# Layer 0 of a graph network: filter taps split in batches through memory, and the elementwise work of a pair rearranged over four engines

## What is computed

```
norm = (row sums of adj + 1e-6) ** -0.5
f_hom = adj @ ((x @ theta) * norm) * norm
f_het = x @ W_h
gate  = sigmoid(x @ W_t + b_t)
out   = elu(gate * f_hom + (1 - gate) * f_het)
x1    = layernorm(x + out)
```

## Time and profile before

| | |
|---|---|
| median of 3 runs | 2163.93 us (2160.73 to 2166.66) |
| the profiled execution | 2163.51 us, its span 2161.7 us |
| TensorE, VectorE, ScalarE, GpSimd busy | 91%, 73%, 58%, 20% of the span |
| mean granted TensorE clock | 0.97 of 2.4 GHz |
| DMA over the span | 263 MB, 122 GB/s |

### The profile page before, as it was taken

The page is one execution under the profiler, slowest core; times in us unless marked ns, Lnnn a source line. Parts: engine busy times, 40 slices in busy tenths (PEclk is TensorE's granted clock), DMA queues, the critical chain, the costliest instruction groups (busy, mean ns, idle before and its releaser), DMA issues.

```text
span 2161.7 us, 36678 instructions
## 1 busy us (share of the span) xinstructions
PE 1971.6 (91%) x11270; PEld 1695.5 (78%) x11270; DVE 1583.6 (73%) x2837; ACT 1245.1 (58%) x2303; POOL 425.1 (20%) x370
## 2 busy tenths in 40 slices
PE   6888888887788879994999999999999999999997
PEld 5887777776688868883888888888888888888886
DVE  5999798798577766774777677777777777777674
ACT  6887687786455566663445454545454545545452
POOL 5887687685000000000000000000000000000000
PEclk9999999998899989996999999999999999999999
DMA  4556566555322268884212121212122121212110
GB/s 145 204 200 209 192 225 218 198 207 218 91 82 79 72 207 263 255 265 152 76 52 92 46 91 45 91 46 90 60 77 77 59 81 55 88 49 91 62 40 20
DMA packets 174943, 263.25 MB, mean 122 GB/s; under 512 B 13250, under 2 KB 125608, under 8 KB 170632
## 3 DMA queue, kind: packets, MB, share of 16 engines
q1 hardware_dynamic: 174856, 262.29, 35.9%
HBM read 174.16 MB, written 88.08 MB: 121 GB/s over the span
## 4 chain that ended last, share of the span: by engine, by line
PE 51%; issue 1%; DVE 1%; DMA 1%; ACT 1%; SPq 0%; POOLq 0%; POOL 0%; ACTq 0%; DVEq 0%
PE c_ps_g L1431 37%; PE c_ps_m L1412 4%; PE c_ps_s L1412 2%; PE c_ps_m L1440 2%; PE c_ps_y L1466 1%; PE c_ps_m L1442 1%; PE c_ps_y L1510 1%; PE c_ps_m L1510 1%; PE c_ps_s L1494 1%; PE c_ps_m L1441 1%; DMA c_yf<-y_spec 1%; PE c_ps_m L1511 0%; PE c_ps_y L1511 0%; DVE c_wi_l L1377 0%; ACT c_yo L1143 0%
## 5 line engine op out<-in xcount | busy, mean ns | idle before, releaser
L1215 POOL TENSOR_TENSOR c_rstd<-c_var_eps,c_neg_half 128x4 f32<-128x4 f32 x32 | 32.2, 1008 | 1131.7 <-DVE c_var_eps L1331 1131.7
L1431 PE MATMUL c_ps_g<-c_xh,c_wh_l 128*128 128x512 f32 x384 | 155.3, 405 | 0.0
L1431 PE MATMUL c_ps_g<-c_nh,c_wi_l 128*128 128x512 f32 x384 | 153.3, 399 | 0.0
L1431 PE MATMUL c_ps_g<-c_xl,c_wh_h 128*128 128x512 f32 x384 | 151.8, 395 | 0.0
L1431 PE MATMUL c_ps_g<-c_xh,c_wh_h 128*128 128x512 f32 x384 | 151.7, 395 | 0.0
L1431 PE MATMUL c_ps_g<-c_ch,c_wi_l 128*128 128x512 f32 x384 | 151.6, 395 | 0.0
L1431 PE MATMUL c_ps_g<-c_ch,c_wi_h 128*128 128x512 f32 x384 | 151.6, 395 | 0.0
L1431 PE MATMUL c_ps_g<-c_nh,c_wi_h 128*128 128x512 f32 x384 | 151.5, 395 | 0.0
L1431 PE MATMUL c_ps_g<-c_cl,c_wi_h 128*128 128x512 f32 x384 | 151.5, 395 | 0.0
L1431 PE MATMUL c_ps_g<-c_nl,c_wi_h 128*128 128x512 f32 x384 | 151.5, 395 | 0.0
L837 PE MATMUL m_ps<-m_wh,m_xl 128*128 128x256 f32 (+1 forms) x406 | 131.8, 325 | 20.7 <-DVE m_wl L817 20.6
(11 more groups left out here) (228 smaller groups left out, 6658.9 us busy)
## 6 DMA issues: line engine op xcount, KB each, us to landing
w_spec<-a_spec SPq DMA_DIRECT2D x32, 1088.0 KB, 11.0
m_w<-w_spec SPq DMA_DIRECT2D x34, 1024.0 KB, 7.5
a_xt<-in_x_t SPq DMA_DIRECT2D x64, 256.0 KB
a_xn<-in_x_n SPq DMA_DIRECT2D x64, 256.0 KB, 9.4
x_t<-a_x1t SPq DMA_DIRECT2D x64, 256.0 KB, 9.5
s_x<-x_t SPq DMA_DIRECT2D x64, 256.0 KB, 3.0
y_spec<-m_y SPq DMA_DIRECT2D x64, 256.0 KB, 5.6
c_x<-x_t SPq DMA_DIRECT2D x32, 512.0 KB, 4.1
```

What stands on the lines that cost most here:

```text
L1431: last = nc.tensor.matmul(out, stationary, moving, start=(count == 0), stop=(count == total - 1))
```

## The change

The taps no longer come in three copies per pair. In every fourth step SyncE loads the taps of four pairs at once over all 128 partitions (`tr`), ScalarE makes the high part (`th`) and VectorE the low part (`tl`), and three steps later SyncE stores high, low and high into a scratch tensor in memory (`taps_s`). From there it loads for each pair the 102 stacked rows (`gs`, now four buffers), in its step i for pair i-7. The spectra matmuls of a pair move from two steps after its load to six and seven steps after, and the stores of the finished spectra move back by as much.

The powers for the norm and for the normalisation become one power of four columns, in GpSimd's step i for pairs i-2 and i-6; the variance's epsilon is added by VectorE. The gate is written back to where it was in PSUM and read there by VectorE; the mix reads het in PSUM (the copy of het stays, for the difference). The normalisation becomes an instruction with three operands, the third a broadcast column. The clamp becomes a minimum with zero on GpSimd, and the exponential loses its sign. ScalarE's, GpSimd's, VectorE's and TensorE's instructions stand in another order in the step. In the product stage two semaphores of ScalarE become one, and VectorE's subtraction for x loses its own signal.

```diff
-def phase_a(nc, G, x_n, x_t, adj_t, w0, b_t, masks, x1_t, taps, dft_w, w_spec):
+def phase_a(nc, G, x_n, x_t, adj_t, w0, b_t, masks, x1_t, taps, taps_s, dft_w, w_spec):
...
+    TB = 4
+    TC = 2 * TAPS * TB * 4 * P // P
...
-        gr = sb("gr", [ROWS, RING, 4, P])
-        gh = sb("gh", [ROWS, 4, P], F32R)
-        gs = sb("gs", [ROWS, 2, 4, P], F32R)
+        tr = sb("tr", [P, TC])
+        th = sb("th", [P, TC], F32R)
+        tl = sb("tl", [P, TC], F32R)
+
+        gs = sb("gs", [ROWS, RING, 4, P], F32R)
...
-                    reached(sp, s_gs, i - RING + 1)
-                    for copy in range(3):
-                        sp.dma_start(gr[copy * 2 * TAPS:(copy + 1) * 2 * TAPS, r].rearrange("p c k -> p (c k)"),
-                                     taps[:, bass.ts(i, 4 * P)]).then_inc(s_in[r], 16)
+                    if n % TB == 0:
+                        m = k * (UNROLL // TB) + n // TB
+                        here = taps[bass.ds(m, 1)]
+                        reached(sp, s_tl, m)
+                        sp.dma_start(tr[:, :], here.rearrange("o p c -> (o p) c")).then_inc(s_tr, 16)
                 if live(4):
                     p = i - 4
                     reached(sp, s_res, p - 1)
                     sp.dma_start(xn[:, u], x_n[:, bass.ts(p, 2 * D)].rearrange("p (b d) -> p b d", b=2)).then_inc(s_xn[u], 16)
-                piece = n % 8 - 4
-                if 0 <= piece < PIECES and live(5 + piece):
-
-                    p = i - 5 - piece
-                    half = (n - 5 - piece) % 16 // 8
-                    reached(sp, s_gw, 4 * (p + 1))
-                    sp.dma_start(w_spec[bass.ds(2 * k - half, 1), :, piece * PL:piece * PL + PL].rearrange("o p d c -> (o p) d c"),
+                    if n % TB == 0:
+                        m = k * (UNROLL // TB) + n // TB - 1
+                        here = taps_s[bass.ds(m, 1)]
+                        reached(sp, s_tl, m + 1)
+                        for copy, part in enumerate((th, tl, th)):
+                            sp.dma_start(here[:, copy].rearrange("o (p c) -> (o p) c", p=P), part[:, :].bitcast(F32)).then_inc(s_ts, 16)
+                if live(7):
+                    q, r = i - 7, (n - 7) % RING
+                    m, at_step = k * (UNROLL // TB) + (n - 7) // TB, (n - 7) % TB
+                    here = taps_s[bass.ds(m, 1)]
+
+                    reached(sp, s_ts, 48 * (m + 1))
+                    sp.dma_start(gs[:, r].rearrange("p c k -> p (c k)").bitcast(F32),
+                                 here.rearrange("o h (r x c) -> (o h r) x c", x=TB, c=4 * P)[:, at_step]).then_inc(s_gs[r], 16)
+                piece = n % 8 - 1
+                if 0 <= piece < PIECES and live(10 + piece):
+
+                    q = i - 10 - piece
+                    half = (n - 10 - piece) % 16 // 8
+                    reached(sp, s_gw, 4 * (q + 1))
+                    sp.dma_start(w_spec[bass.ds(2 * k - 2 + half, 1), :, piece * PL:piece * PL + PL].rearrange("o p d c -> (o p) d c"),
                                  spec[:, half, piece * PL:piece * PL + PL]).then_inc(s_spec[half], 16)
...
-                    reached(act, s_mix, p + 1)
-                    reached(act, s_ex, p)
-                    nc.scalar.activation(below[:, :, :], mix[:, u], ACT.Relu, scale=-1.0).then_inc(s_below, 1)
                     reached(act, s_below, p + 1)
                     reached(act, s_res, p)
-                    nc.scalar.activation(ex[:, :, :], below[:, :, :], ACT.Exp, scale=-1.0).then_inc(s_ex, 1)
+                    nc.scalar.activation(ex[:, :, :], below[:, :, :], ACT.Exp).then_inc(s_ex, 1)
...
+                if live(7):
+                    spectra_out(i - 7, 3, 7)
+                if live(1):
+                    p = i - 1
+                    r = (n - 1) % RING
                     reached(act, s_hom, p - 1)
                     nc.scalar.activation(ah[:, v], at[:, r], ACT.Copy).then_inc(s_ah, 1)
                 if live(2):
-                    spectra_out(0)
-                if live(1):
-                    p = i - 1
-                    reached(act, s_gs, p)
-                    nc.scalar.activation(gh[:, :, :], gr[:, (n - 1) % RING], ACT.Copy).then_inc(s_gh, 1)
-                if live(2):
                     f_high(0)
-                    spectra_out(1)
+                if live(6):
+                    spectra_out(i - 6, 0, 6)
+                if live(1) and n % TB == 1:
+                    m = k * (UNROLL // TB) + n // TB
+                    reached(act, s_tr, 16 * (m + 1))
+                    reached(act, s_ts, 48 * m)
+                    nc.scalar.activation(th[:, :], tr[:, :], ACT.Copy).then_inc(s_th, 1)
+                if live(2):
                     f_high(1)
-                    spectra_out(2)
                     reached(act, s_mix, p2 - 1)
                     nc.scalar.activation(het[:, u], ps_hh[:, 2 * u:2 * u + 2, D:2 * D], ACT.Copy).then_inc(s_het, 1)
+                if live(6):
+                    spectra_out(i - 6, 1, 6)
...
-                if live(5):
-                    p = i - 5
-                    reached(act, s_mv, p + 1)
-                    reached(act, s_rstd, p)
-                    nc.scalar.activation(var_eps[:, :], mv[:, v, :, 1], ACT.Identity, bias=eps[:, 0:1]).then_inc(s_ve, 1)
                 if live(2):
                     reached(act, s_gp, p2 + 1)
-                    reached(act, s_gd, p2 - 1)
-                    nc.scalar.activation(gate[:, u], ps_g[:, :, :], ACT.Tanh, scale=0.5).then_inc(s_gate, 1)
-                    spectra_out(3)
+                    nc.scalar.activation(ps_g[:, :, :], ps_g[:, :, :], ACT.Tanh, scale=0.5).then_inc(s_gate, 1)
+                if live(6):
+                    spectra_out(i - 6, 2, 6)
...
-                if live(2):
-                    p = i - 2
-                    reached(pool, s_dege, p + 1)
-                    reached(pool, s_diff, p - 1)
-                    reached(pool, s_fl, p - 1)
-                    nc.gpsimd.tensor_tensor(norm[:, u], deg_eps[:, :], neg_half[:, :], ALU.pow).then_inc(s_norm, 1)
+                if live(2) or live(6):
+
+                    if live(2):
+                        reached(pool, s_dege, i - 1)
+                        reached(pool, s_diff, i - 3)
+                        reached(pool, s_fl, i - 3)
+                    if live(6):
+                        reached(pool, s_ve, i - 5)
+                        reached(pool, s_x1, i - 7)
+                    these = slice(0 if live(2) else 2, 4 if live(6) else 2)
+                    nc.gpsimd.tensor_tensor(roots[:, u, these], sums_eps[:, u, these], neg_half[:, these], ALU.pow).then_inc(s_root, 1)
                 if live(1):
                     p = i - 1
                     reached(pool, s_xh, p + 1)
                     reached(pool, s_gp, p - 1)
                     nc.gpsimd.tensor_tensor(xl[:, v], xt[:, (n - 1) % RING], xh[:, v].bitcast(F32), ALU.subtract).then_inc(s_xl, 1)
-                    reached(pool, s_ah, p + 1)
-                    reached(pool, s_hom, p - 1)
-                    nc.gpsimd.tensor_tensor(al[:, v], at[:, (n - 1) % RING], ah[:, v].bitcast(F32), ALU.subtract).then_inc(s_al, 1)
...
                     nc.gpsimd.tensor_tensor(res[:, u], ex[:, :, :], xn[:, u], ALU.add).then_inc(s_res, 1)
-                if live(5):
-                    p = i - 5
-                    reached(pool, s_ve, p + 1)
-                    reached(pool, s_x1, p - 1)
-                    nc.gpsimd.tensor_tensor(rstd[:, v], var_eps[:, :], neg_half[:, :], ALU.pow).then_inc(s_rstd, 1)
+                if live(1):
+                    p = i - 1
+                    reached(pool, s_ah, p + 1)
+                    reached(pool, s_hom, p - 1)
+                    nc.gpsimd.tensor_tensor(al[:, v], at[:, (n - 1) % RING], ah[:, v].bitcast(F32), ALU.subtract).then_inc(s_al, 1)
+                if live(3):
+                    p = i - 3
+                    pool.wait_ge(s_k, 3)
+                    reached(pool, s_mix, p + 1)
+                    reached(pool, s_ex, p)
+                    nc.gpsimd.tensor_scalar(below[:, :, :], mix[:, v], 0.0, None, ALU.min).then_inc(s_below, 1)
...
                     reached(dve, s_deg, p2 + 1)
-                    reached(dve, s_norm, p2)
-                    nc.vector.tensor_scalar(deg_eps[:, :], ps_deg[:, :, 0], 1e-6, None, ALU.add).then_inc(s_dege, 1)
+                    reached(dve, s_root, p2 - 1)
+                    nc.vector.tensor_scalar(sums_eps[:, u, 0:2], ps_deg[:, :, 0], 1e-6, None, ALU.add).then_inc(s_dege, 1)
...
-                if live(3):
-                    reached(dve, s_gd, p3)
-                    reached(dve, s_hom, p3 + 1)
-                    reached(dve, s_het, p3 + 1)
-                    for b in range(2):
-                        last = nc.vector.scalar_tensor_tensor(diff[:, b], ps_hom[:, b], norm[:, v, b:b + 1], het[:, v, b],
-                                                              ALU.mult, ALU.subtract)
```

(85 more changed lines are left out.)

65 lines of the change are left out of this document (29 added, 36 removed).

## The result

The changed kernel takes 2211.14 us (2210.14 to 2215.21, four runs), the kernel before on the same chip 2162.75. The ratio is 1.0222, 95% interval 1.0205 to 1.024: slower by 48 us, where 2130 was forecast, and outside the range of 2099 to 2170. The next stage's first load goes out at 589.00 and not at 542.71, 46 us later; behind it both spans are nearly alike (1621.2 and 1619.0 us in the profiled executions). So nearly the whole loss lies in layer 0.

What follows compares the result with a forecast made beforehand. Layer 0 was taken as bound by VectorE's 7.54 us step plus 0.47 of DMA backlog. 60 steps from 7.99 to 7.33 (-39.6), start -4.4, end +10.8: -33 from 2163.5 gives 2130 us, range 2099 to 2170.

Steps and rivals of the forecast that it cites:

- Two periods are 3.95 + 4.95 + 0.65 + 0.1 + T: Layer 0's stacked-load loop, two steps: 3.95 behind TensorE's wait, 4.95 to residual's end, 0.65 to issue, T, 0.1; period 7.33 us.
- T: Stacked load's time from issue to landing: 3.9 us plain, 5.8 and 6.1 behind the three stores, mean 5.0 over even steps.
- 5.7, up to 6.5: VectorE's microseconds per layer 0 step after the change, forecast to fall under TensorE's 6.6.
- Odd steps have less and follow: In layer 0, the even steps' mean T of 5.0 us sets the period; odd steps wait less and follow.
- The end: Layer 0's drained steps and last spectra stores, to the next stage: 28.9 us in place of 18.1, so 10.8 more.
- the start: Layer 0's first steps: no early wait for taps and four steps without spectra matmuls, 4.4 us earlier at step 6.
- Late load: Rival: stacked load runs as narrow as the old taps, T 2.5 us longer in every step, period 8.58, 2205 us; chance 0.22.
- Hidden load: Rival: the stacked load never delays TensorE, whose 6.65 us a step, with 0.2 for the gate, holds; 2101 us; chance 0.22.
- VectorE does not get faster: Rival: normalisation stays at 1.6 and mix at 1.05, 6.8 us a step, still under 7.33; no effect; no chance given.
- GpSimd slower than costed: Rival: clamp over 1.3 us, residual ends 0.5 later, period 7.6, 2146 us; chance 0.14, shared with other small waits.
- The mix near 0.7, no wait of ScalarE for taps, the gate in PSUM at no cost, nothing in the multiply stage: Smaller claims: mix from 1.05 to about 0.7 us, ScalarE not waiting for taps, gate 0 to 0.2, multiply stage nothing.
- Steps of 7.2 to 7.6 and none of 9 to 13: Sign to look for in layer 0's steps: all at 7.2 to 7.6 us, no long ones.

Runs made afterwards that it cites:

- e4_both: Changed kernel with the stacked taps loaded one step earlier and the variance's epsilon added by ScalarE instead of VectorE: 2116.15 us, ratio 0.9769.
- e3_ve_scalar: Changed kernel with only the addition of the variance's epsilon moved back from VectorE to ScalarE: 2187.2 us, ratio 1.0095.
- g2_three_operand_ve: Changed kernel with VectorE's addition of the variance's epsilon in a three-operand form, same place and value: 2203.22 us, ratio 1.0186.

## Why the prediction was wrong

**The step that failed: "Two periods are 3.95 + 4.95 + 0.65 + 0.1 + T", with a mean T.** T itself was right: in 17 of the 18 waits of TensorE for it the load took 4.9 to 5.8 us from issue to matmul, 5.6 in most, where I had 5.8 and 6.1 behind stores; in one plain step it took 4.64, where I had 3.9. What failed is the rest of the sum, for the two steps with the stores, and its being the limit at all, for the other two. By it two steps take 15.5 to 15.8 us with the stores and 13.6 to 13.9 without, 29.3 for four. Measured are 18.2 (6.60 and 11.59) and 15.5 (7.46 and 8.05), 33.7.

*The fixed part: 2.7 us every four steps.* Between VectorE's first instructions at 210.04 and 228.22 the chain is: residual ended 4.3 in, 2.2 to the issue, 5.6 to TensorE, 6.1 behind it, 18.2 in all; mine was 15.5 with T of 5.8. The 0.65 to the issue left out the issuing of the three stores, 1.65 us of SyncE's time, though I had counted their bytes: 1.5 too little. The 3.95 behind the wait, counted to TensorE's next degree matmuls, is right at full clock. In e4_both, without a stall, it is 3.94 in TensorE's timeline:

```profile
159.90 0.36 PE L461 MATMUL a_ps_w<-a_dw,a_gs 102*128 102x272 f32 x1
...
163.84 0.17 PE L478 MATMUL a_ps_t<-a_ones,a_al 128*128 128x2 f32 x1
```

In the changed kernel it is 5.54 (222.14 to 227.68), 1.6 more: the time at half clock after the stall, which I had not costed. T was 0.3 shorter than mine. The 4.95 up to the residual was right too: VectorE's first instruction stands 0.54 behind the degree, where nothing delays it, so the 4.3 is 4.9 from there.

*VectorE: 1.7 us every four steps.* "5.7, up to 6.5", under TensorE's 6.6: it was 7.46, since a tiny instruction costed at 0.1 took 1.0 beside GpSimd. I applied the contention to the long instruction and not to the short one, whose wait is what is left of GpSimd's instruction, whatever its own length.

*The shape.* "Odd steps have less and follow" spread the wait over all steps. By the runs three steps stand at a limit of their own and the fourth takes the whole wait. Averaging over four steps is not what made the forecast too low. It hid that by my own sum one step in four would take some 9 us (15.5 to 15.8 less 6.65), and with it the stall and its half clock.

The sum: 59 steps of 1.21 more are 71, of which the two parts above give some 64 and the loop's two jumps, costed at nothing, some 8. The end 18.0 and not 10.8 makes 7, the start 2.6 at step 6 and not 4.4 makes 2: 2130 + 80 = 2210, the time measured.

- *Late load, the rival on the other side* (2205, chance 0.22): right in place, but that its mean period of 8.58 meets the measured 8.54 is luck. Its reason, a T of 7.5 in every step from a narrow rate, was wrong. The rule of the Trainium skill (DMA: Bandwidth & Descriptors, section "Why a DMA increments its semaphore by 16 and not by 1") spoke against that T, and the landings of 4.6 to 5.8 us agree with it; that the rival "would fall" with it was my error.
- *Hidden load* (2101): false as built, true one step earlier.
- *VectorE does not get faster, "it changes nothing"*: the mix fell as forecast, but VectorE was the limit of the plain steps all the same, and that was worth 24 us (e3_ve_scalar).
- *GpSimd slower than costed*: the minimum was, 1.60; its loop of 6.3 busy still fits 6.6. My upper bound of 6.6 was added up wrong: 0.45, 1.3, 1.25, 1.7, 1.15 and 1.3 are 7.15 (degree, power, low part of x, residual, low part of adj, clamp).
- *The mix near 0.7, no wait of ScalarE for taps, the gate in PSUM at no cost, nothing in the multiply stage*: the first two show in the trace, for the others nothing speaks against it, but neither was run by itself.
- *The end*: drained steps with four spectra each took 4.7 us, at a granted clock of 0.50 (565 to 575 us) and with TensorE waiting for ScalarE's copy before most of them, where I had 3.2. The last stores took 13.0 us, for 12.4.
- *"Steps of 7.2 to 7.6 and none of 9 to 13"*: one in four was of 9 to 13, with a wait of 2.1 to 3.9. I had not asked what one bad step in four does.

## What to carry to other kernels

Cost the steps of a cycle one by one, each with the limit that holds in it, and not as one mean period. Count the issuing queue's own time for whatever stands ahead of a load. A load that TensorE uses in order wants a whole step of slack; here moving three lines was worth 85 us. Before a small instruction moves to VectorE, look at what GpSimd runs at that moment.

## What the runs showed of the hardware

A VectorE instruction on 128x2 in SBUF takes 0.16 us alone (549.87 in the changed kernel). Beside a GpSimd instruction with two SBUF inputs it takes up to 1.21 in that kernel, and in both forms it ends 0.01 to 0.04 us behind it (the changed kernel, g2_three_operand_ve). After a stall of 3.5 us TensorE's granted clock was 0.50 for some 3 us, and the work behind the stall took 1.6 us more than in e4_both. The jumps back of a loop of 16 long steps cost 6.7 and 7.6 us in e4_both, with all engines held up (10.5 and 11.6 in the kernel before), and code written out does not have them.
